# Ranks and counts of edges on TensorE with reads in runs, heads in two buffers, tiles evenly spaced, 858 gather columns

## The chip, the core and the metric

The kernel runs on one core of a Trainium2 chip. The metric is the device time of one execution in microseconds. TensorE multiplies, VectorE, ScalarE and GpSimd work on vectors, SyncE (SP) issues DMAs; each takes its instructions in order, and they wait for one another through semaphores. GpSimd issues the indirect DMAs (gathers and scatters of rows).

## The reference, cut to what matters

```
x: (6250, 256) f32; src, dst: (100000,) int32, sorted by dst; edge_weight: (100000,)
xn = layernorm(x)
agg = segment_sum(xn[dst] * edge_weight[:, None], src, 6250)
gnn = relu((xn + agg) @ W1 + b1) @ W2 + b2               # 256 -> 512 -> 256
k, v = per-head layernorms of xn (8 heads of 32, own weights and biases)
mix = per head q @ (k.T @ v / N), q = xn;  + xn
x = x + gnn + mix
z = layernorm(x)
top 2 of 16 experts of z @ gate_w + gate_b, softmax of the two values
moe = sum of weight * (relu(z @ w1[e] + b1[e]) @ w2[e] + b2[e])   # 256 -> 512 -> 256
out = x + layernorm(z + moe) * gamma + beta
```

## The kernel before, in words

Nodes are padded to 49 buckets of 128 rows (`NT`), a bucket being the high part of `src`. The kernel is a row of blocks; within a block each engine has its own program, and a barrier stands between blocks.

**First block.** The 100,000 edges lie in SBUF as 128 partitions by 28 groups of 28 (`EC` = 784 columns, written `(g j)`). `bkt_f` holds each edge's bucket. It is counted how many edges of each group fall in each bucket: VectorE makes for every bucket a 0/1 matrix of 784 columns (`matches`, L774), TensorE adds them up over partitions and positions with 28 matmuls of 196 columns for seven buckets (`count`, L628), VectorE copies the counts (L778). Each edge also needs its rank among the edges of the same partition, group and bucket: for every distance d from 1 to 27 GpSimd subtracts bucket numbers d positions apart (L591), ScalarE squares and applies relu(1 - x), so that equal buckets give 1 (L671, L675), GpSimd adds that to `rank` (L596). From the counts VectorE makes prefix sums, writes each edge's start by a predicated copy for every bucket (L859 mask, L862 copy of the starts, L867), adds `rank` (L874) and gets each edge's place. The edges are then sorted into records of eight (`QE`), group by group: VectorE builds matrices (`matrices`), ScalarE weights them and normalizes x, TensorE multiplies (L650), GpSimd scatters the records to DRAM (L606).

**Second block, the gather loop.** The records are `ET` = 864 columns of 128 edges, in 432 pairs. GpSimd gathers the 128 rows of xn of a column in one indirect DMA (L1278), twelve pairs of places in a ring; SP lets a pair go when its place is free (`release`, L1149). The other engines run in *units*: 480 of them (432 pairs, 48 of which are used twice where a pair crosses a bucket's end, rounded up to a multiple of 6). In a unit VectorE selects rows by edge (L1422, twice), TensorE multiplies (L1303, L1304), VectorE adds into the bucket's sums (L1439). TensorE may be four units ahead of VectorE (`SUMB`). Further work hangs on unit numbers, written into the program when it is generated:

- *heads*, seven groups of seven tiles at `heads_from[g]` = 9, 19, 29, 38, 48, 58, 68: xn is loaded into `xn_rows`, VectorE centres it into `nd` (`heads_centre`), ScalarE squares, VectorE sums, takes the root's inverse and scales (`heads_norm`, four units on), TensorE makes k.T v (`head_sums`, four units on, L1314), VectorE adds (`heads_add`, nine units on).
- *tiles* (slots), one for each of the 49 buckets, at `turn_unit[s]`, when the bucket's sums are done: transposes, MLP, attention, residual, norm, gate, choice of two experts over 13 units, then the ranks of the choices; ScalarE writes marks for the expert lists (`mark`, L1235 to L1238).

**Third block.** Lists of tokens by expert are made of the marks; SP loads weights of the first four experts (L1692, L1696). **Fourth block.** 114 tiles of 128 tokens go through their experts (gather L1842, TensorE L1863, L1884), SP loads the other twelve experts' weights. **Last block.** Mixing, norm, output.

Of the kernel before, what the change touches and what calls it, by code (L numbers as in the profile page):

```python
# [58 lines left out]
def gps_layer(nc, x, src, dst, edge_weight, gW1, gb1, gW2, gb2, klw, klb, vlw, vlb,  # L59
# [32 lines left out]
    ET = -(-(NGRP * ((GC * P + NT * (QE - 1)) // QE)) // (TQ * ROUND)) * ROUND  # L92
    EROUNDS = ET // ROUND

# [15 lines left out]
    assert EP % PB == 0 and RB <= BU  # L110
# [9 lines left out]
    rec_dram = nc.dram_tensor("edge_records_sorted", [ET * TQ + NGRP * NQ * P, QW], F32).ap()  # L120
# [10 lines left out]
    with ctx:  # L131
# [47 lines left out]
        apart = [early(EC) for _ in range(3)]  # L179
        early = carver(row_hot[1], GC * P)  # L180
        rank = early(EC)
        same = [early(EC) for _ in range(3)]
# [39 lines left out]
        starts = [carve(NGRP) for _ in range(4)]  # L222
# [3 lines left out]
        later = lambda a, d: bg2(a)[:, :, d:]  # L226
# [16 lines left out]
        edge_sel = edge_sel.rearrange("p (s n) -> p s n", n=P)  # L243
        tile_rows = nd[:, 0:BT * P * REC].rearrange("p (c s w) -> p c s w", c=BT, w=REC)
# [30 lines left out]
        zeros = carve(ET * REC)  # L275
# [194 lines left out]
        s_local = sem("local_ranks")  # L470
# [37 lines left out]
        with nc.Block() as block:  # L508
            @block.sync
            def _(sp):  # L510
# [11 lines left out]
                sp.dma_start(rec_dram[0:ET * TQ, :].rearrange("(p z) w -> p (z w)", p=P), zeros).then_inc(s_recz, 16)  # L522
# [35 lines left out]
            def _(pool):  # L558
# [13 lines left out]
                pool.iota(aside, pattern=[[NQ * P, NGRP]], base=ET * TQ, channel_multiplier=0,  # L572
# [12 lines left out]
                pool.memset(rank, 0.0).then_inc(s_local, 1)  # L585
                pool.wait_ge(s_bkt, 1)
                for d in range(1, GC + 2):
                    if d < GC:
                        if d > 3:
                            pool.wait_ge(s_same, d - 3)  # L590
                        pool.tensor_tensor(later(apart[d % 3], d), later(bkt_f, d), bg2(bkt_f)[:, :, 0:GC - d],  # L591
                                           ALU.subtract).then_inc(s_gap, 1)
                    if d >= 3:
                        pool.wait_ge(s_same, d - 2)
                        pool.wait_ge(s_local, d - 2)
                        pool.tensor_tensor(later(rank, d - 2), later(rank, d - 2), later(same[(d - 2) % 3], d - 2),  # L596
                                           ALU.add).then_inc(s_local, 1)

# [18 lines left out]
            def _(pe):  # L617

                pe.wait_ge(s_upto, 1)

                def count(j, k):
                    r, p, _ = tile_at(j, k)
                    pe.wait_ge(s_match, r * GT + GT)
                    if over(r - 1):
# [6 lines left out]
                run_steps(pe, count, 0, NR - 1, 1, (NR - 1) // 2)  # L631
# [35 lines left out]
            def _(act):  # L667

                for d in range(1, GC):
                    act.wait_ge(s_gap, d)  # L670
                    act.activation(later(apart[d % 3], d), later(apart[d % 3], d), ACT.Square).then_inc(s_gapsq, 1)  # L671
                    act.wait_ge(s_gapsq, d)
                    if d > 3:
                        act.wait_ge(s_local, d - 2)
                    act.activation(later(same[d % 3], d), later(apart[d % 3], d), ACT.Relu, bias=1.0, scale=-1.0).then_inc(s_same, 1)  # L675

# [62 lines left out]
            def _(dve):  # L739
# [17 lines left out]
                dve.wait_ge(s_dve, n.add(P // HD + 1))  # L757
                dve.tensor_copy(bkt_f, bkt_i).then_inc(s_bkt, 1)
                dve.wait_ge(s_bkt, 1)

                dve.tensor_scalar(src_i, src_i, P - 1, None, ALU.bitwise_and).then_inc(s_dve, 1)
                dve.wait_ge(s_dve, n.add())
                dve.scalar_tensor_tensor(code, dst_i, float(P), src_i, ALU.mult, ALU.add).then_inc(s_dve, 1)
                dve.wait_ge(s_dve, n.add())

                dve.wait_ge(s_consts, 8)
                dve.tensor_tensor(upto_b, before[:], ident[:], ALU.add).then_inc(s_upto, 1)

                def matches(j, k):
                    r, p, _ = tile_at(j, k)  # L770
                    if looped(r) or r < NR:

                        for i in range(GT):
                            dve.tensor_scalar(match[p][:, i * EC:(i + 1) * EC], bkt_f, iota_n[:, ds(r * GT + i, 1)], None,  # L774
                                              ALU.is_equal).then_inc(s_match, 1)
                    if over(r):
                        dve.wait_ge(s_counted, r)
                        dve.tensor_copy(cnt[:, ds((r - 1) * (GT * NGRP), GT * NGRP)],  # L778
                                        bank[1 - p][:, 0:GT * NGRP]).then_inc(s_cnt, 1)

                run_steps(dve, matches, 0, NR, 1, (NR - 1) // 2)


# [11 lines left out]
                dve.memset(restart, 1.0).then_inc(s_dve, 1)  # L795
                dve.wait_ge(s_dve, n.add())
# [1277 lines left out]
```

## Time and profile before

| | |
|---|---|
| three runs | 2380.33, 2381.49 (median), 2381.5 us |
| the profiled execution | 2381.34 us, span 2379.1 us |
| TensorE busy | 1638.3 us (69%), mean granted clock 0.849 |
| VectorE busy | 1453.1 us (61%) |
| GpSimd busy | 1391.3 us (58%) |
| ScalarE busy | 739.9 us (31%) |
| DMA | 233.44 MB, mean 98 GB/s |

The span is the time from the first to the last instruction of the profiled execution. Busy time is averaged over stages that have different limits, so the stretches are read one by one. A granted clock of 1.00 is TensorE at 2.4 GHz, 0.50 is 1.2 GHz.

### The profile page before, as it was taken

The page shows a single profiled execution, that of the slowest core. Times are in us where ns is not written, and L with a number is a line of the kernel's source. Part 1 is how long each engine was busy: PE and PEld are TensorE (multiplying, and loading weights), DVE is VectorE, ACT ScalarE, POOL GpSimd, SP SyncE. Part 2 cuts the span into 40 slices and gives each one's busy share as a digit, 9 for nine tenths or more (in the row PEclk, how much of TensorE's full clock was granted, in tenths as well). Part 3 has the DMA queues.
Part 4 walks back from the last instruction along what each step waited for, and adds up shares of the span by engine and source line. Part 5 has one row for each costly group of instructions (what it writes and reads, how often), then busy time and mean ns, then how long its engine had stood idle before and what let it go on. Part 6 is the DMA issues. An engine that isn't in the chain of part 4 may idle for free. (4 is left out here: it accounts for less than half of the span.)

```text
span 2379.1 us, 40341 instructions
## 1 busy us (share of the span) xinstructions
PE 1638.3 (69%) x9284; PEld 1371.2 (58%) x9285; DVE 1453.1 (61%) x4177; ACT 739.9 (31%) x2173; POOL 1391.3 (58%) x1512
## 2 busy tenths in 40 slices
PE   5602788624556887787878777776569999999900
PEld 2202777613555776676766656654468888888800
DVE  8499988637676666666665665654343443434379
ACT  4803789500000344322222222221213333333200
POOL 8001788748876776677777777776225554555400
PEclk9856899856778999898898889888679999999955
DMA  4000011254333444344444444447581111111184
GB/s 153 0 0 16 20 35 34 20 104 134 115 113 89 133 127 120 108 128 120 127 121 125 124 119 125 124 118 98 77 288 57 62 62 57 60 61 61 52 290 149
DMA packets 133498, 233.44 MB, mean 98 GB/s; under 512 B 28775, under 2 KB 85199, under 8 KB 133374
## 3 DMA queue, kind: packets, MB, share of 16 engines
q0 software_dynamic: 56384, 145.17, 22.8%
q1 hardware_dynamic: 49294, 61.00, 8.4%
q10 hardware_dynamic: 27696, 25.83, 3.4%
q8 instruction: 51, 0.84, 0.1%
q14 instruction: 73, 0.60, 0.1%
HBM read 189.48 MB, written 42.43 MB: 97 GB/s over the span
## 5 line engine op out<-in xcount | busy, mean ns | idle before, releaser
L1278 POOL DMA_INDIRECT lower<-xn_rows,lower x864 | 865.0, 1001 | 310.5 <-issue 239.3
L1303 PE MATMUL bank<-lower 128*128 x960 | 342.9, 443 | 145.4 <-SPq L1154 121.3
L1439 DVE TENSOR_TENSOR xh<-xh,bank 128x256 f32 x480 | 199.7, 416 | 285.9 <-PE bank L1304 285.1
L1422 DVE TENSOR_SCALAR lower<-iota_n,lower 128x128 f32<-128x128 f32 x960 | 294.4, 357 | 69.7 <-issue 56.2
L606 POOL DMA_INDIRECT edge_records_sorted<-lower x112 | 200.8, 1793 | 205.1 <-ACT lower L717 174.9
L1304 PE MATMUL bank<-lower 128*128 x960 | 320.5, 419 | 0.0
L1303 PEld LDWEIGHTS bank<-lower 128*128 128x128 f32 x960 | 177.7, 213 | 212.1 <-issue 200.0
L650 PE MATMUL bank<-lower 128*64 128x128 f32 x1568 | 189.8, 285 | 125.1 <-ACT lower L701 120.8
L650 PEld LDWEIGHTS bank<-lower 128*64 128x64 f32 x1568 | 183.6, 145 | 128.8 <-DVE lower L915 121.4
L1834 POOL DMA_INDIRECT expert_rows<-arena,dest_idx x114 | 114.6, 1005 | 213.7 <-DVE arena L1929 196.5
L1920 DVE TENSOR_SCALAR arena<-bank,b_tile 128x128 f32<-128x128 f32 x456 | 128.4, 344 | 178.4 <-PE bank L1863 178.4
L1863 PEld LDWEIGHTS bank<-arena 128*128 128x128 f32 x1824 | 225.9, 195 | 6.0
L1304 PEld LDWEIGHTS bank<-lower 128*128 128x128 f32 x960 | 206.1, 215 | 35.1
L1863 PE MATMUL bank<-arena 128*128 128x128 f32 x1824 | 226.3, 278 | 0.0
L1884 PE MATMUL bank<-upper,arena 128*128 x912 | 225.9, 391 | 0.0
L1884 PEld LDWEIGHTS bank<-upper,arena 128*128 128x128 f32 x912 | 165.3, 191 | 29.6 <-issue 3.6
L701 ACT ACTIVATE lower<-lower 128x32 f32<-128x32 f32 x784 | 169.3, 309 | 9.3 <-DVE lower L900 8.4
L1901 ACT ACTIVATE arena<-lower 128x1024 f32 x114 | 120.5, 1057 | 60.9 <-issue 60.9
L1929 DVE COPY arena<-bank 128x256 f32<-128x256 f32 x114 | 48.4, 424 | 144.0 <-PE bank L1884 144.0
L1907 ACT ACTIVATE arena<-bank 128x256 f32<-128x256 f32 x114 | 43.7, 383 | 289.4 <-PE bank L1873 289.4
L1842 POOL DMA_INDIRECT arena<-xn_rows,tok_idx x114 | 109.5, 960 | 38.7 <-issue 32.2
L1216 ACT ACTIVATE std<-mv,eps_col 128x1 f32<-128x1 f32 x49 | 14.4, 295 | 320.1 <-DVE mv L1589 319.0
(316 smaller groups left out, 2530.4 us busy)
## 6 DMA issues: line engine op xcount, KB each, us to landing
lower<-xn_rows,lower POOLq DMA_INDIRECT x864
lower<-in_L_ffn_w SPq DMA_DIRECT2D x16, 512.0 KB, 9.7
upper<-in_L_ffn_w SPq DMA_DIRECT2D x16, 512.0 KB, 10.5
xn_rows<-xh SPq DMA_DIRECT2D x7, 896.0 KB, 4.1
arena<-xn_rows ACTq DMA_DIRECT2D x7, 896.0 KB, 5.5
lower<-xn_rows ACTq DMA_DIRECT2D x49, 128.0 KB
xn_rows<-lower ACTq DMA_DIRECT2D x49, 128.0 KB
x_plus_beta<-lower ACTq DMA_DIRECT2D x49, 128.0 KB
```

Of the source, the lines that this page charges most:

```text
L606: pool.indirect_dma_start(rec_dram, bass.IndirectOffsetOnAxis(quad_idx[i][:, c:c + 1], 0), quads[i][:, c * QW:(c + 1) * QW], None).then_in ...
L650: mm = pe.matmul(bank[6 + p][0:NQ * QW, 0:P], moving[p][:, e].rearrange("p c w -> p (c w)"), row_hot[p][:, e, :], start=e == 0, stop=e == ...
L701: done = act.activation(moving[p][:, e, :, 1], col_hot[p][:, e, :], ACT.Copy, scale=group_wgt[p][:, e:e + 1])
L1278: pool.indirect_dma_start(edge_rows[:, t % ROUND, :], None, xn_dram, bass.IndirectOffsetOnAxis(source.bitcast(U32)[:, t:t + 1], 0)).then_i ...
L1303: pe.matmul(sums_at(u), edge_sel[:, 2 * u % ESEL, :], rows_flat[:, ds(at, D)], start=True, stop=False)
L1304: pe.matmul(sums_at(u), edge_sel[:, (2 * u + 1) % ESEL, :], rows_flat[:, ds(at + D, D)], start=False, stop=True).then_inc(s_sum, 1)
L1422: dve.tensor_scalar(edge_sel[:, (2 * u + h) % ESEL, :], iota_n[:], lane[:, at:at + 1], weight_s[:, at:at + 1], ALU.is_equal, ALU.mult).the ...
L1439: dve.tensor_tensor(xh[:, at], xh[:, at], sums_at(u), ALU.add).then_inc(s_acc, 1)
L1863: mm = pe.matmul(bank[2 + p][:, m * P:(m + 1) * P], w1_tile[p][:, c * F + m * P:c * F + (m + 1) * P], tokT[p][:, c * P:(c + 1) * P], start ...
L1884: mm = pe.matmul(bank[6 + p][:, 0:D], hidT[p][:, m * P:(m + 1) * P], upper[:, ds(e * (FC * D) + m * D, D)], start=False, stop=m == FC - 1)
L1901: act.activation(w1_tile[p], lower[:, ds(e * (DC * F), DC * F)], ACT.Copy).then_inc(s_w1t, 1)
L1920: dve.tensor_scalar(hidT[p][:, m * P:(m + 1) * P], bank[2 + p][:, m * P:(m + 1) * P], b1_tile[:, ds(t + m * XT, 1)], 0.0, ALU.add, ALU.max ...
```

## The change

**Counts.** A copy of the buckets in the order `(j g)`, `bkt_c`, is what the matches are made of. For one position c the count's matmul now reads 28 neighbouring elements for each of seven buckets; before it read elements 28 apart. The loops are written out.

```
-                    matched = match[p].rearrange("p (b g j) -> p b g j", g=NGRP, j=GC)
+                    matched = match[p].rearrange("p (b j g) -> p b j g", g=NGRP, j=GC)
                     for c in range(GC):
-                        mm = pe.matmul(bank[p][:, 0:GT * NGRP], upto_b, matched[:, :, :, c], start=c == 0, stop=c == GC - 1)
+                        mm = pe.matmul(bank[p][:, 0:GT * NGRP], upto_b, matched[:, :, c, :], start=c == 0, stop=c == GC - 1)
```

**Ranks.** GpSimd's subtractions and additions go. TensorE makes the difference of two positions as a sum of two matmuls, with the identity and with minus the identity, and adds the equal ones into banks 6 and 7; ScalarE reads the difference from PSUM.

```
+                def differences(d):
+                    if d > 2:
+                        pe.wait_ge(s_gapsq, d - 2)
+                    for h, lo, hi in halves_from(d):
+                        to = bank[2 + 2 * (d % 2) + h][:, 0:hi - lo]
+                        pe.matmul(to, ident_b, bkt_c[:, lo:hi], start=True, stop=False)
+                        mm = pe.matmul(to, minus_b, bkt_c[:, lo - d * NGRP:hi - d * NGRP], start=False, stop=True)
+                    mm.then_inc(s_gap, 1)
+                def add_same(d):
+                    pe.wait_ge(s_same, d)
+                    for h, lo, hi in halves_from(d):
+                        mm = pe.matmul(bank[6 + h][:, lo - h * EH:hi - h * EH], ident_b, same[d % 2][:, lo:hi],
+                                       start=False, stop=hi - lo == NGRP)
+                    mm.then_inc(s_local, 1)
...
+                differences(1)
+                differences(2)
+                for d in range(1, GC):
+                    add_same(d)
+                    if d + 2 < GC:
+                        differences(d + 2)
+                    if d % 4 == 3:
+                        count(d // 4)
```

```
-                    act.activation(later(apart[d % 3], d), later(apart[d % 3], d), ACT.Square).then_inc(s_gapsq, 1)
+                    if d > 2:
+                        act.wait_ge(s_same, d - 2)
+                    for h in range(2):
+                        lo, hi = max(d * NGRP, h * EH), (h + 1) * EH
+                        if lo < hi:
+                            sq_done = act.activation(apart[d % 2][:, lo:hi], bank[2 + 2 * (d % 2) + h][:, 0:hi - lo], ACT.Square)
+                    sq_done.then_inc(s_gapsq, 1)
```

On TensorE, at its program's start, `xh` holds the match matrices and `lower` the buckets and the rank matrices. Before:

```order
L628 MATMUL bank0<-xh,lower 128x196 [waits bucket_matches,prefix_matrix_made]
L628 MATMUL bank0<-xh,lower 128x196 x27
L628 MATMUL bank1<-xh,lower 128x196 [waits bucket_matches]
L628 MATMUL bank1<-xh,lower 128x196 x27
L435 UNCONDITIONAL_BRANCH
```

and now, from the differences of distance 4 over the addition of distance 3 and the differences of distance 5 to the first count (the numbers of lines are those of the changed kernel):

```order
L627 MATMUL bank2<-lower 128x280 [waits bucket_gaps_squared]
L628 MATMUL bank2<-lower 128x280
L627 MATMUL bank3<-lower 128x392
L628 MATMUL bank3<-lower 128x392
L634 MATMUL bank6<-lower 128x308 [waits same_buckets]
L634 MATMUL bank7<-lower 128x392
L627 MATMUL bank4<-lower 128x252 [waits bucket_gaps_squared]
L628 MATMUL bank4<-lower 128x252
L627 MATMUL bank5<-lower 128x392
L628 MATMUL bank5<-lower 128x392
L645 MATMUL bank0<-xh,lower 128x196 [waits bucket_matches]
L645 MATMUL bank0<-xh,lower 128x196 x27
```

A count of 28 matmuls stands behind every fourth distance, and each distance waits for ScalarE (`same_buckets`, `bucket_gaps_squared`).

**VectorE of the first block.** The scans' restart columns are written by GpSimd at the start, not by VectorE between its steps. The loop over buckets is written out and reads the starts in place (no L862). The ranks are added from the two banks in two instructions.

```
-                            dve.tensor_copy(starts[k % 4], start[:, ds((r * GT + k) * NGRP, NGRP)]).then_inc(s_dve, 1)
...
+                        dve.copy_predicated(bg2(pos), bg2(masks[(b - 1) % 4]), start[:, (b - 1) * NGRP:b * NGRP].unsqueeze(2)
+                                            .to_broadcast([P, NGRP, GC])).then_inc(s_dve, 1)
```

**Columns.** `ET` is 858, not 864; the zeroed part of the records stays 864 columns (`ZT`). There are 429 pairs and still 480 units.

```
-    ET = -(-(NGRP * ((GC * P + NT * (QE - 1)) // QE)) // (TQ * ROUND)) * ROUND
-    EROUNDS = ET // ROUND
+    ET = -(-(NGRP * ((GC * P + NT * (QE - 1)) // QE)) // (2 * TQ)) * 2
+    ZT = -(-ET // 8) * 8
```

**Heads.** Groups use `nd` and `xn_rows` in turn, and are centred in place; a group is loaded when the sums of the group two before are done. TensorE's sums come eight units on, VectorE's addition thirteen.

```
+        head_rows = lambda g: nd if g % 2 else xn_rows
-                            if u == heads_from[g] + 4 + k // 2:
+                            if u == heads_from[g] + 8 + k // 2:
                                 head_sums(g, k)
-                        if u == heads_from[g] + 9:
+                        if u == heads_from[g] + 13:
                             heads_add(g)
```

**Tiles.** They begin at units 88, 96, 103, 111, 118, ..., 7.5 apart until tile 34, where before they began at 88, 93, 98, 102, 107, ..., 4.67 apart until tile 15; from 34 on the numbers are the same (343, 352, ...), the last 482. `stage_h` comes one unit earlier, `mark` two units later and behind the unit's other work; the last `mark` goes to the third block, beside VectorE's work there.

```
-        turn_unit = [max(slots_from + 1 + -(-14 * s // 3), done_by[s + 1] + 2) for s in range(NT)]
+        turn_unit = [max(slots_from + 1 + -(-15 * s // 2), done_by[s + 1] + 2) for s in range(NT)]
```

**Weights.** In the third block SP loads one expert's weights, and the next four in the fourth, when the second token tile has landed.

```
-                for e in range(WAHEAD):
-                    sp.dma_start(w1_sb[:, e], w1[e].rearrange("(c p) f -> p c f", p=P)).then_inc(s_we[e], 16)
...
+                sp.dma_start(w1_sb[:, 0], w1[0].rearrange("(c p) f -> p c f", p=P)).then_inc(s_we[0], 16)
...
+                    if e == 0:
+                        sp.wait_ge(s_tok[1], 16)
+                        for later in range(1, WAHEAD):
+                            load_weights(sp, later)
```

On SP, before, around the barrier into the fourth block (`lower` holds w1, `upper` w2):

```order
L1692 DMA lower<-in_L_ffn_w 128x2x512 x4
L1696 DMA upper<-in_L_ffn_w 128x4x256 [waits tiles_listed] x4
L1807 UNCONDITIONAL_BRANCH [waits barrier_Pool_Activation_PE_DVE_SP_release]
L1685 DMA lower<-in_L_ffn_w 128x2x512 [waits weights_of_expert0]
L1686 DMA upper<-in_L_ffn_w 128x4x256
```

and now:

```order
L1720 DMA lower<-in_L_ffn_w 128x2x512
L1722 DMA upper<-in_L_ffn_w 128x4x256 [waits tiles_listed]
L1839 UNCONDITIONAL_BRANCH [waits barrier_Pool_Activation_PE_DVE_SP_release]
L1714 DMA lower<-in_L_ffn_w 128x2x512 [waits weights_of_expert0,rows_landed1]
L1715 DMA upper<-in_L_ffn_w 128x4x256
L1714 DMA lower<-in_L_ffn_w 128x2x512
```

Six of the eight transfers stand behind the barrier and behind the landing of the second token tile (`rows_landed1`).

## Rows read from the trace of the kernel before

**Rows 1.** The page's first line.
```profile
span 2379.1 us, 40341 instructions
```
**Rows 2.** Time line of TensorE to 250 us: start us, us, engine, line.
```profile
35.46 56.70 PE L628 MATMUL bank<-xh,lower 128*128 128x196 bf16 x168 [0.49 <-DVE xh L774]
92.71 1.92 PE L638 MATMUL bank<-xh,lower 128*128 128x476 f32 x2 [0.55 <-DVE xh L778]
```
**Rows 3.** Busy us (instructions) of PE, PEld, DVE, ACT, POOL; clock; DMA.
```profile
540.00:760.00 220.00, 124.83 (x579) 107.30 (x579) 149.35 (x295) 13.62 (x14) 167.22 (x139) 0.75 0.37 113
860.00:1000.00 140.00, 110.85 (x609) 93.95 (x606) 92.01 (x379) 56.32 (x154) 87.33 (x93) 0.91 0.40 117
1000.00:1630.00 630.00, 490.29 (x2304) 395.98 (x2305) 385.82 (x1484) 159.52 (x443) 478.36 (x498) 0.88 0.42 123
```
**Rows 4.** Waits (us in total, times, longest): 1000:1630, then 540:760 twice, 860:1000.
```profile
POOL lower L1278 <- SPq L1149: 11.0, 36, 0.3
...
POOL lower L1278 <- SPq L1149: 13.6, 12, 4.1
...
PE bank L1314 <- DVE lower L1470: 92.2, 7, 16.5
...
POOL lower L1278 <- SPq L1149: 29.5, 18, 5.4
```
**Rows 5.** Time line of TensorE near the gather loop's end.
```profile
1684.07 1.22 PE L1303 MATMUL bank<-lower 128*128 x2 [2.11 <-SPq L1154]
...
1687.40 1.22 PE L1303 MATMUL bank<-lower 128*128 x2 [1.26 <-SPq L1154]
```
**Rows 6.** Time line of TensorE in the third block.
```profile
1732.05 0.21 PE L1712 MATMUL bank<-lower,upper 128*128 128x114 bf16 x1
1732.10 0.21 PE L1711 MATMUL bank<-lower,upper 128*128 128x114 bf16 x1
```
**Rows 7.** Time line of ScalarE: ranks, and a copy from PSUM later.
```profile
12.09 0.83 ACT L671 ACTIVATE lower<-lower 128x756 f32<-128x756 f32 x1 [10.01 <-POOL lower L591]
...
64.03 0.26 ACT L671 ACTIVATE lower<-lower 128x28 f32<-128x28 f32 x1
...
1664.80 0.38 ACT L1222 ACTIVATE lower<-bank 128x256 f32<-128x256 f32 x1 [1.19 <-PE bank L1364]
```
**Rows 8.** Time line of VectorE in the first block.
```profile
104.83 1.20 DVE L795 MEMSET xh<- 128x1372 f32 x1 [0.35 <-DVE xh L792]
...
137.57 0.42 DVE L859 TENSOR_SCALAR xh<-lower,iota_n 128x784 uint16<-128x784 bf16 x1 [0.25 <-DVE upper L848]
...
139.33 0.41 DVE L859 TENSOR_SCALAR xh<-lower,iota_n 128x784 uint16<-128x784 bf16 x1
139.66 0.17 DVE L862 COPY xh<-xh 128x28 f32 x1
139.74 1.02 DVE L867 COPY_PREDICATED xh<-xh 128x784 f32<-128x784 uint16 x1
140.66 0.41 DVE L859 TENSOR_SCALAR xh<-lower,iota_n 128x784 uint16<-128x784 bf16 x1
...
147.70 0.42 DVE L859 TENSOR_SCALAR xh<-lower,iota_n 128x784 uint16<-128x784 bf16 x1 [0.46 <-DVE xh L867]
```
**Rows 9.** Time line of VectorE: additions of two units without waits.
```profile
527.43 0.41 DVE L1439 TENSOR_TENSOR xh<-xh,bank 128x256 f32 x1
...
528.27 0.41 DVE L1439 TENSOR_TENSOR xh<-xh,bank 128x256 f32 x1
```
**Rows 10.** Time line of ScalarE at the second block's end.
```profile
1716.58 0.40 ACT L1235 ACTIVATE upper<-iota_n,upper 128x128 f32<-128x128 f32 x1 [4.69 <-DVE upper L1639]
...
1718.80 0.48 ACT L1238 ACTIVATE upper<-upper 128x128 f32 x1
```
**Rows 11.** Time lines of GpSimd and TensorE at the fourth block's start.
```profile
1742.89 0.97 POOL L1842 DMA_INDIRECT arena<-xn_rows,tok_idx  x1 [0.82 <-POOL tok_idx L1828]
...
1750.21 0.66 PE L1873 MATMUL bank<-ident,arena 128*128 128x128 f32 x2 [11.05 <-DMA arena<-xn_rows,tok_idx]
```

More of the change, by code:

```diff
@@ L109, in gps_layer @@
     BT = -(-ET // P)
[L110 removed]
+    assert RB <= BU and ZT * TQ % P == 0
     WAHEAD = 4
@@ L581, in _ @@
                                    pattern=[[0, P]], channel_multiplier=1).then_inc(s_consts, 1)
[L585 to L597, printed above, removed]
+                for a, first in ((restart_g, bg(restart_g)[:, :, 0:1]), (restart_b, gb(restart_b)[:, :, 0:1])):
+                    pool.memset(a, 1.0).then_inc(s_poolc, 1)
+                pool.wait_ge(s_poolc, 6)
+                for a, first in ((restart_g, bg(restart_g)[:, :, 0:1]), (restart_b, gb(restart_b)[:, :, 0:1])):
+                    pool.memset(first, 0.0).then_inc(s_restart, 1)
                 def scatter(r, i):
@@ L617, in _, with halves_from @@
             def _(pe):
-                pe.wait_ge(s_upto, 1)
-                def count(j, k):
-                    r, p, _ = tile_at(j, k)
+                pe.wait_ge(s_bkt, 2)
+                pe.wait_ge(s_upto, 3)
+                def halves_from(d):
+                    return [(h, max(d * NGRP, h * EH), (h + 1) * EH) for h in range(2) if d * NGRP < (h + 1) * EH]
+                def differences(d):
[6 more added lines that the diff above has]
+                    mm.then_inc(s_gap, 1)
@@ L629, in count @@
                     mm.then_inc(s_counted, 1)
-                run_steps(pe, count, 0, NR - 1, 1, (NR - 1) // 2)
+                for h in range(2):
+                    cols = slice(h * EH, (h + 1) * EH)
+                    pe.matmul(bank[6 + h][:, 0:EH], ident_b, bkt_c[:, cols], start=True, stop=False)
+                    pe.matmul(bank[6 + h][:, 0:EH], minus_b, bkt_c[:, cols], start=False, stop=False)
+                differences(1)
[6 more added lines that the diff above has]
+                        count(d // 4)
@@ L876, in _ @@
+                dve.wait_ge(s_dve, n.back(0))
+                dve.wait_ge(s_local, GC - 1)
+                for h in range(2):
+                    cols = slice(h * GC // 2, (h + 1) * GC // 2)
+                    dve.tensor_tensor(by_column(pos_i)[:, cols, :], by_column(pos)[:, cols, :],
+                                      bank[6 + h][:, 0:EH].rearrange("p (j g) -> p j g", g=NGRP), ALU.add).then_inc(s_dve, 1)
+                dve.wait_ge(s_dve, n.add(2))
                 dve.tensor_scalar(part_i, pos_i, QSHIFT, P - 1, ALU.arith_shift_right, ALU.bitwise_and).then_inc(s_dve, 1)
@@ L1245, in _ @@
                 load(0)
-                with act.Fori(0, NG - 1) as g:
+                for g in range(NG):
                     heads(g)
-                heads(NG - 1)
                 act.wait_ge(s_kv, DC)
```

187 lines of the change are left out of this document (96 added, 91 removed).

## The prediction

> **What bounds the kernel now.** I read the page first, then the time lines of each engine in the first stage, the busy time by stretch, and the waits in the gather loop. The profiled execution has a span of 2379.1 us [rows 1] and took 2381.34 us, 2.2 us more than its span; the median of the three runs shown is 2381.49 us, so the sum below, made against 2381.3, stands for the median too. No engine bounds the whole; the stages follow each other and each has its own limit.
>
> In the first stage TensorE counts: 168 matmuls of 196 columns run without a break from 35.46 to 92.16 us, 0.337 us each, and the prefix matmuls start at 92.71 us [rows 2]. VectorE only builds what they read; GpSimd and ScalarE make the ranks meanwhile and are done near 64 us, off the path. From 92.7 us to the sort at 220 us VectorE alone sets the pace.
>
> In the gather loop (512 to 1698 us) GpSimd sets the pace. From 1000 to 1630 us it issues 498 gathers, one per 1.265 us [rows 3], and its 36 waits for a free place come to 11.0 us, 0.30 us each, which is what issue costs anyway [rows 4]. In three places it waits longer. From 540 to 760 us (the heads) 12 such waits hold 13.6 us, 10.0 above issue, and TensorE stands 92.2 us in seven waits for the normed heads [rows 4]. From 860 to 1000 us (tiles at every 4.67 units) 18 waits hold 29.5 us, 24.1 above issue [rows 4]. At the end a pair of gathers is used every 3.33 us instead of 2.53 [rows 5].
>
> **First stage.** The new count reads 7 runs of 28 neighbouring elements where the old one took single elements 28 apart. The trace has no such read. Bounds: a bf16 matmul on 114 neighbouring columns starts every 0.05 us [rows 6], 0.44 ns a column, twice that at the half clock, so 196 columns cost 0.086 or 0.17 us; at the other end stands the old read, 0.337 us [rows 2]. I take the run price, since 27 of 28 steps go to the next element: 196 matmuls in 17 us.
>
> The Trainium skill, page "SBUF — State Buffer", section "Door 1: The DMA port swizzle", says that reads which hit one 16-byte line at least twice run at full bandwidth and that each step to a new line pays. The old read's 0.337 us [rows 2] agrees with it; by that rule the new read is cheap and the time is the forecast's, and if each of its columns paid as before it would be about 2342 us.
>
> New on TensorE are the ranks: for each of 27 distances the difference of bucket numbers (two matmuls, in two halves) and the addition (one). The widths 784-28d add up to 10,584; three times that and 4 x 392 is 33,320 columns, with the counts 71,736: 31.5 us at the full clock, 60 at the half. ScalarE squares from two banks and applies Relu. From 0.83 us for 756 columns and 0.26 for 28 an instruction is 0.24 us and 0.78 ns a column, and reading a bank is no dearer (0.38 us for 256) [rows 7]: 67 instructions, 32.7 us. The engines hand over at every distance. Distances 1 to 13 are ScalarE's: 39 x 0.24 us + 15,288 x 0.78 ns = 21.3 us. From 14 on ScalarE has 11.3 us and TensorE, with four of the seven counts, 13.5; a narrow distance is shorter than a count, so little overlaps: 14 to 25 us. TensorE can start at about 12.2 us. At the full clock the stage ends between 48 and 58 us; I take 58, with the handovers. At the half clock TensorE alone needs 60, and the stage ends at 72 to 83, say 80. TensorE is busy two thirds of it; a stretch with 57% busy shows clock 0.75 and one with 79% shows 0.91 [rows 3], so I take 0.82 and an end at 62. Against 92.7 that is **-30.7** (-12 to -35). VectorE's 49 matches, 0.41 us each like the bucket loop's comparisons [rows 8], are hidden behind the counts; without that cover a round of seven would cost 2.9 us.
>
> Behind it VectorE loses two memsets of 1.20 us and two small ones [rows 8]: **-2.6**, with nothing beside them. The loop over the buckets starts a round of seven every 10.13 us (137.57 to 147.70), with 1.33 us from bucket to bucket and a stall at each round's end [rows 8]. Without the copy of the start (0.08 us from its start to the next) a bucket is 1.25 us, and no round ends: 49 x 1.25 + 0.5 instead of 7 x 10.13, less 0.3 for the addition that is now two: **-8.8**. The sort and all up to the gathers move forward unchanged.
>
> **Gather loop.** Heads: TensorE comes to the head sums at unit 8 behind the centring, not 4, and leads VectorE by four units at most, so the norm (unit 4) is done when it comes. The 92.2 us of waits go, and **-10** of GpSimd's with them. VectorE's long instructions stay, and so, I think, does the dearer gather there (167.22/139 = 1.20 us against 478.36/498 = 0.96 [rows 3]). The earlier group's products are added at unit 13, which is the next group's third or fourth, before its sums; the load waits for the buffer two groups back, long summed. If a buffer came late, the 10 us would return.
>
> Tiles: at 4.67 units GpSimd runs out of places; at 9.75 (1000 to 1630) never. The new 7.5 lies between. From 860 to 1000 us 93 gathers are 51.7 units [rows 3], 2.71 us a unit, 12.7 us a tile. A unit alone costs VectorE 0.84 us [rows 9], so a tile 8.8 us. At 7.5 units that is 15.1 of the 17.1 us that GpSimd needs for its 13.5 gathers: it fits with 12% to spare, for 34 tiles instead of 16. I leave 2 us of waits: **-22** (0 to -24). Tiles from 34 on stand where they stood, so the last ends no later.
>
> Columns: 858 instead of 864 are three pairs fewer, at the end, where a pair costs 3.33 us [rows 5]: **-10** (not below 3 x 2.53 = 7.6). There are still 480 units; the last three repeat a pair.
>
> **End of the loop and experts.** The last marks on ScalarE run from 1716.58, where VectorE's last instruction lets them go, to 1719.28 us, the end of the block [rows 10]. Moved past the barrier they lie beside VectorE's making of the high places: **-2.7**, and if that cover failed nothing is lost, for they would stand where they do now. One expert's weights are loaded there instead of four. The first token gather is issued by 1743.86 us and used at 1750.21 [rows 11], with the weights of twelve experts under way. Without them at most some 4 of these 6.35 us go; the three experts' weights that come later lie beside the first tiles and take some of it back. Net **-2** (-6 to +5).
>
> Sum: 30.7 + 2.6 + 8.8 + 10 + 22 + 10 + 2.7 + 2 = 88.8, and 2381.3 - 88.8 = 2292.5, said as **2293 us**.
>
> **Rivals.**
> 1. The clock stays at half in the first stage. For it: TensorE and ScalarE take turns, and a stretch with breaks shows 0.75 [rows 3]; against it: the breaks are under 2 us each, and the loop's stretches with such breaks show 0.9. The stage ends at 80, not 62: 2311 us. The Trainium skill ("TensorE: Matmul & The Clock Gate", "What's actually happening") has the array held at half by default and released by activity; it allows either here, and no row decides.
> 2. Runs cost as much as single elements: 196 x (0.337 - 0.086) = 49 us more, 2342 us. For it: no row has a broken run. Against it: the 0.05 us of [rows 6].
> 3. At 7.5 units the loop is still full. If a unit cost 2 us instead of 0.84, a tile would cost 3.3, and 7.5 units 18.3 us against 17.1: 1.2 us lost on each of 33 tiles, 40 us of waits in place of 2. Half of that is likelier: the 22 us are given back, 2315 us.
> 4. The late weights hold the experts up. Expert 1 is wanted some seven tiles on; if its weights or the tokens beside them delay the tiles by 10 us net: 2305 us.
> 5. Slower than before: broken runs cost more than single elements, because each of the seven runs restarts the read. It decides from 0.086 + 88/196 = 0.54 us a matmul; at 0.60 the time is 2394 us. No matmul of 196 columns in the trace costs more than the old one's 0.337 us.
>
> **How the numbers follow.** The forecast with its own spread (2280 to 2304) gets 0.63, rival 1 0.10, rival 2 0.06, rival 3 0.09, rival 4 0.07, rival 5 0.02, and 0.03 is left for what I have not seen. The range 2278 to 2325 holds the forecast, rivals 1 and 4 and most of rival 3, and leaves out 2, 5 and the rest. A difference of 0.2% (4.8 us) is about what can be told from none. Faster by more: 0.97; within it: 0.01; slower: 0.02.
>
> **What would show it.** Count matmuls near 0.09 us and the prefix matmuls at about 62 us; the bucket loop in 62 us; no wait for normed heads on TensorE; a gather every 1.27 us from the end of the heads to the last columns, without waits for places; 858 gathers; no ScalarE instruction behind VectorE's last at the barrier; the first token used in about 3 us. I am wrong if the counts cost 0.3 us, if the granted clock of the first stage is near 0.5, or if waits for places come back between tiles.

## The result, and the profile after

The changed kernel takes 2280.89 us (median of four runs, 2278.57 to 2282.12) where the old one takes 2380.91 in the same job: a ratio of 0.9584, with a 95% interval of 0.9567 to 0.9602. That is 100 us less; 88.8 were forecast. The profiled execution took 2280.35 us with this span:

```profile
span 2278.6 us, 40242 instructions
```

Of TensorE in the first stage, the time line (start us, us, engine, line) answers to [rows 2]:

```profile
43.24 2.52 PE L645 MATMUL bank<-xh,lower 128*128 128x196 bf16 x28
...
46.78 0.25 PE L634 MATMUL bank<-lower 128*128 128x168 bf16 x1 [0.57 <-ACT lower L710]
...
51.10 2.52 PE L645 MATMUL bank<-xh,lower 128*128 128x196 bf16 x28
54.24 1.04 PE L667 MATMUL bank<-xh,lower 128*128 128x476 f32 x2 [0.62 <-DVE xh L814]
```

28 counts in 2.52 us are 0.090 us each, against 0.337 before. The prefix matmuls start at 54.24 instead of 92.71. The same stretch in the view of windows (busy us and instructions of PE, PEld, DVE, ACT, POOL; granted clock; DMA share; GB/s) and in the groups by line (count, busy us, mean ns, idle ahead):

```profile
12.00:54.00 42.00, 34.65 (x318) 26.05 (x316) 19.15 (x55) 29.22 (x81) 0.00 (x0) 1.00 0.50 148
```
```profile
L805 DVE TENSOR_SCALAR xh<-lower,iota_n 128x784 bf16<-128x784 bf16 x49 | 16.8, 417 | 0.0
L710 ACT ACTIVATE lower<-lower 128x756 bf16<-128x756 bf16 (+26 forms) x27 | 14.3, 530 | 0.9
...
L634 PE MATMUL bank<-lower 128*128 128x392 bf16 (+13 forms) x40 | 9.1, 284 | 7.0 <-ACT lower L710 6.8
```

The clock is 1.00, TensorE is busy 34.65 of 42 us, and its waits for ScalarE are 6.8 us in all. (The trace's first record of the clock begins at 15.95 us; ahead of it the view reads 1.00 for want of a record, and matmuls of 392 columns start 0.33 us apart there, 0.17 later: the half clock.) VectorE behind it, to be read beside [rows 8]:

```profile
93.61 0.76 DVE L883 TENSOR_SCALAR xh<-lower,iota_n 128x784 uint16<-128x784 bf16 x2
...
95.21 0.41 DVE L883 TENSOR_SCALAR xh<-lower,iota_n 128x784 uint16<-128x784 bf16 x1
...
154.90 1.64 DVE L896 TENSOR_TENSOR xh<-xh,bank 128x392 int32<-128x392 f32 x2
```

With the copies between them that is a bucket every 1.25 us and no break: the loop takes 61.3 us. In the gather loop, first the waits of GpSimd from 540 to 760 us, then from 860 to 1000, beside [rows 4]:

```profile
POOL lower L1305 <- SPq L1174: 2.7, 9, 0.3
...
POOL lower L1305 <- SPq L1174: 4.3, 14, 0.3
```

Both are 0.3 us a wait, what issue costs. The windows answer to [rows 3]:

```profile
1000.00:1500.00 500.00, 387.92 (x1959) 311.20 (x1957) 315.51 (x1233) 142.03 (x402) 378.90 (x398) 0.94 0.43 127
...
1540.00:1580.00 40.00, 23.51 (x88) 16.91 (x89) 14.86 (x55) 6.22 (x18) 22.04 (x24) 0.78 0.93 88
```

In the last 40 us of gathers DMA is busy 0.93 of the time and moves less (88 GB/s) than at 0.43 before: something else is slow there. GpSimd's and ScalarE's time lines from there to the third block, which is GpSimd's iota:

```profile
457.32 0.95 POOL L1305 DMA_INDIRECT lower<-xn_rows,lower  x1 [0.30 <-issue]
...
1576.95 0.94 POOL L1305 DMA_INDIRECT lower<-xn_rows,lower  x1 [0.30 <-issue]
1616.45 0.24 POOL L1726 IOTA lower<- 128x114 f32 x1 [38.57 <-POOLq L1149]
1639.21 0.18 POOL L1864 CAST tok_idx<-rows_all 128x1 uint32<-128x1 f32 x1 [22.51 <-POOLq L1717]
1640.21 0.97 POOL L1878 DMA_INDIRECT arena<-xn_rows,tok_idx  x1 [0.82 <-POOL tok_idx L1864]
```
```profile
1594.13 0.40 ACT L1265 ACTIVATE upper<-iota_n,upper 128x128 f32<-128x128 f32 x1 [0.31 <-issue]
...
1596.35 0.48 ACT L1268 ACTIVATE upper<-upper 128x128 f32 x1
1596.73 0.40 ACT L1228 ACTIVATE lower<-xh 128x256 f32 x1
...
1610.42 0.48 ACT L1268 ACTIVATE upper<-upper 128x128 f32 x1
1610.81 0.36 ACT L1252 ACTIVATE lower<-bank 128x256 f32<-128x256 f32 x1
...
1651.07 1.06 ACT L1937 ACTIVATE arena<-lower 128x1024 f32 x1 [4.38 <-SPq L1843]
```

Two things show that I had not foreseen. Marks (L1265 to L1268) run right ahead of the last tile's staging of h (L1228) and of its last norm's copy (L1252), which start the moment they end. And ScalarE waits 4.38 us at 1651.07 for SP's word that an expert's weights are there.

Read at the same places of both traces, the difference adds up like this (negative is saved):

| stretch | before | after | difference |
|---|---|---|---|
| start to the prefix matmuls | 92.71 | 54.24 | -38.5 |
| from there to the first sort matrix | 120.3 | 106.3 | -14.0 |
| from there to the first gather (512.03, 457.32) | 299.1 | 296.8 | -2.2 |
| gathers 0 to 166 | 255.9 | 241.4 | -14.5 |
| gathers 166 to 250, 350 to 830 | 715.4 | 709.4 | -6.0 |
| gathers 250 to 350 | 149.2 | 126.0 | -23.2 |
| gather 830 to the last's end | 54.5 | 43.7 | -10.8 |
| last gather's end to the third block | 32.4 | 38.6 | +6.2 |
| third block | 22.3 | 22.8 | +0.5 |
| fourth block's start to the end of the span | 637.2 | 639.4 | +2.2 |

The sum is -100.3; the spans differ by 100.5.

### The profile page after: what moved, and what is told of

Its sections match the earlier page's. It is cut to its first block and busy times, and to the rows that moved or that the text cites. A ratio compares the mean times of both kernels' runs of the same rounds, so it can differ in the third digit from the quotient of the medians.

```text
span 2278.6 us, 40242 instructions
## 1 busy us (share of the span) xinstructions
PE 1603.1 (70%) x9408; PEld 1348.5 (59%) x9409; DVE 1416.2 (62%) x4128; ACT 731.0 (32%) x2186; POOL 1326.7 (58%) x1455
## 5 line engine op out<-in xcount | busy, mean ns | idle before, releaser
L1305 POOL DMA_INDIRECT lower<-xn_rows,lower x858 | 850.6, 991 | 270.2 <-issue 238.5
L1330 PEld LDWEIGHTS bank<-lower 128*128 128x128 f32 x960 | 169.2, 209 | 318.3 <-issue 307.9
L1331 PEld LDWEIGHTS bank<-lower 128*128 128x128 f32 x960 | 204.3, 213 | 35.3
L1943 ACT ACTIVATE arena<-bank 128x256 f32<-128x256 f32 x114 | 43.8, 384 | 285.1 <-PE bank L1909 285.1
## 6 DMA issues: line engine op xcount, KB each, us to landing
upper<-in_L_ffn_w SPq DMA_DIRECT2D x16, 512.0 KB, 10.5
```

Source lines behind the costliest of these rows:

```text
L1305: pool.indirect_dma_start(edge_rows[:, t % ROUND, :], None, xn_dram, bass.IndirectOffsetOnAxis(source.bitcast(U32)[:, t:t + 1], 0)).then_i ...
L1330: pe.matmul(sums_at(u), edge_sel[:, 2 * u % ESEL, :], rows_flat[:, ds(at, D)], start=True, stop=False)
L1331: pe.matmul(sums_at(u), edge_sel[:, (2 * u + 1) % ESEL, :], rows_flat[:, ds(at + D, D)], start=False, stop=True).then_inc(s_sum, 1)
```

## The experiments

Ratios are against the kernel before in the same job. Where I give a difference from the changed kernel I also compare profiled spans, since two jobs' medians differ by a few us.

**The count's read.** The change with matches laid out as before:

```
-  match[..] = (bkt_c == b)          matched = match "p (b j g) -> p b j g";  moving = matched[:, :, c, :]
+  match[..] = (bkt_f == b)          matched = match "p (b g j) -> p b g j";  moving = matched[:, :, :, c]
```

> The changed kernel, with its counts read as before: the matches are laid out group by group, so each count matmul takes 196 single elements 28 apart instead of seven runs of 28. All else stays. My theory, that the read sets the price of a count: 196 matmuls cost 0.337 instead of about 0.087 us, 49 us more on a TensorE that is busy 40 of the stage's 43 us, so the prefix matmuls start near 103 us and the time is about 2330 us (2322 to 2335). Rival: the old stage was long because GpSimd's ranks slowed VectorE's matches and kept TensorE waiting, and the read was not the limit; then the stage ends before 75 us and the time is below 2301 us.

2341.22 us, ratio 0.9819 (0.9793 to 0.9844); the span is 59 us above that of the changed kernel. TensorE's time line, and the window of its end:

```profile
86.60 9.62 PE L645 MATMUL bank<-xh,lower 128*128 128x196 bf16 x28
...
107.63 1.93 PE L667 MATMUL bank<-xh,lower 128*128 128x476 f32 x2 [0.62 <-DVE xh L814]
```
```profile
92.00:106.00 14.00, 13.42 (x47) 5.29 (x46) 1.81 (x3) 8.83 (x40) 0.00 (x0) 0.50 0.00 0
```

The stage ends at 107.6, 53.4 us later, of which the read is 49; the rest is the ranks' matmuls at a lower clock. Up to the first gather another 5.3 us come in: 2.5 behind the prefix matmuls, which still run at the half clock, and 2.8 in the sort, for which I have no cause. The rival is out: the read alone decides whether this stage lasts 54 or 108 us.

**Runs of four.** The groups are split into seven times four, so that a matmul reads 49 runs of 4 neighbours:

```
+  bkt_q = copy of bkt_i, "p (h g j) -> p h j g", g=4;  match[..] = (bkt_q == b)
+  matched = match "p (h j g) -> p h j g", g=4;         moving = matched[:, :, c, :]
```

> The changed kernel, with matches laid out so that a count matmul reads 49 runs of 4 neighbours; one more copy of the bucket numbers (about 1 us) on VectorE. Theory A: each step to an element that is no neighbour costs the 0.337/196 = 1.7 ns of the old read, each step to a neighbour 0.44 ns; then a matmul costs 0.044 * 147/100 + 49 * 1.7 / 1000 = about 0.15 us, and the time is 2281 + 196 * 0.063 + 1 = about 2294 us. Theory B: whatever is read in runs of at least 8 bytes goes at full rate: 0.087 us and 2282 us. Theory C: the read is slow as soon as runs are short: 0.3 us and 2323 us.

2290.87 us, ratio 0.9601 (0.9575 to 0.9627). The count in TensorE's time line:

```profile
28.94 2.70 PE L646 MATMUL bank<-xh,lower 128*128 128x196 bf16 x28
```

28 in 2.70 us are 0.096 us a matmul, against 0.090 in runs of 28 and 0.344 without runs: for the read theory B holds but for 0.006 us, and A and C fall. The Trainium skill, page "SBUF — State Buffer", table row "Cachelines", asks for at least two hits in a 16-byte line; four neighbours of two bytes meet it, and 0.096 us agrees. The total is some 9 us above theory B's: the stage ends at 57.72, 3.5 us later (TensorE starts 2.1 us later behind the added copy, and 196 x 0.006 is 1.2), and the rest, in the sort and the gathers, has no cause that I can name. Over all my runs, but for those of the slow chip below (up to 294), the sort alone took 278 to 283 us from the first scatter to the first gather.

**Counts without the ranks.** The kernel before, only its count changed:

```
+  bkt_c = copy of bkt_i, "p (g j) -> p j g"
-  matches from bkt_f, matched[:, :, :, c]
+  matches from bkt_c, matched[:, :, c, :]      (ranks stay on GpSimd and ScalarE)
```

> The kernel before, with the counts alone changed: bucket numbers are copied into the order column by column, matches follow it, and a count matmul reads seven runs of 28. The ranks stay on GpSimd and ScalarE. My theory now: VectorE's matches cost 1.1 to 1.5 us each while GpSimd makes the ranks and 0.35 us after, so they become the limit and the prefix matmuls start near 72 us instead of 92.7; the time is about 2360 us, and the other 18 us of the changed stage belong to the ranks' move. Rival A, the counts alone explain the stage: it ends near 56 us and the time is 2344 us. Rival B, the read was no limit: 2376 us or more.

2363.35 us, ratio 0.9911 (0.9885 to 0.9937). VectorE's time line, TensorE's wait from 12 to 72 us, TensorE's time line at the end:

```profile
15.78 20.88 DVE L776 TENSOR_SCALAR xh<-lower,iota_n 128x784 bf16<-128x784 bf16 x14
...
63.75 3.18 DVE L776 TENSOR_SCALAR xh<-lower,iota_n 128x784 bf16<-128x784 bf16 x7
```
```profile
PE bank L629 <- DVE xh L776: 43.8, 6, 27.2
```
```profile
70.06 1.04 PE L639 MATMUL bank<-xh,lower 128*128 128x476 f32 x2 [0.54 <-DVE xh L780]
```

A match costs VectorE 1.49 us beside GpSimd's rank operations and 0.45 when they thin out. TensorE now waits 43.8 us for matches, 27.2 of them ahead of its first count, and the stage ends at 70.06: 22.7 us come from the counts alone, the other 15.8 of the 38.5 from moving the ranks, which frees VectorE.

**Tiles.** `turn_unit` with 14/3 in place of 15/2:

> The changed kernel with the tiles again at every 14/3 units behind the first, all else kept. My theory: GpSimd runs out of places in the first 16 tiles as before, 23 us come back in waits: about 2303 us (2300 to 2306), with gathers 250 to 350 taking 149 us instead of 126. Rival: the gain of the even spacing was in part the other edits' (fewer columns, VectorE's shorter operations), and less than 12 us come back: 2293 us or less.

2305.63 us, ratio 0.9671 (0.9645 to 0.9696); the span is 20.1 us longer. Gathers 250 to 350 take 141.3 us instead of 126.0, and GpSimd's waits for places from 800 to 950 us are back:

```profile
POOL lower L1305 <- SPq L1174: 21.0, 19, 5.1
```

The term stands at 15 us, between theory (23) and rival (under 12). The rest of the 20 lies mostly where the tiles' spacing does not reach: 1.6 us ahead of the first gather, 1.6 in the gathers behind 830 and 2.3 among the experts. Before the change the gathers 250 to 350 took 149.2, so that some 8 of their 23 us belong to other edits; which, no run shows.

**The unused records.** The list's end is filled ahead of the sort with zero records, which all name source row 0. Here they name rows 0, 1, 2, ... with weight zero:

```
   pool.wait_ge(s_zero, 1)
+  pool.iota(zeros "p (r w) -> p r w"[:, :, 0], pattern=[[P, ZT]])      # code = 128 * row
```

> The changed kernel, with the unused records at the end of the sorted list naming the source rows 0, 1, 2, ... (weight still zero) where they all named row 0; one more iota on GpSimd in the first stage. The last 28 gathers of the changed kernel take 43.7 us where 28 of the steady ones take 35, DMA is busy 0.97 of that time and moves only 79 GB/s. My theory: that is the price of 128 reads of one row, and with spread rows the last gathers go at GpSimd's pace and their rows land sooner: 2281 - 8.5 - 3 = about 2269 us (2265 to 2273). Rival: it is the number of descriptors or other traffic, and nothing changes: 2281 us.

2264.55 us, ratio 0.9513 (0.9497 to 0.9529), 16.3 us less than the changed kernel. The window of the last gathers of this kernel, then of the changed one:

```profile
1534.00:1569.00 35.00, 27.18 (x129) 21.54 (x129) 17.27 (x68) 6.61 (x19) 26.51 (x28) 0.91 0.40 118
```
```profile
1534.00:1578.00 44.00, 26.18 (x112) 19.25 (x110) 17.42 (x67) 6.62 (x19) 26.63 (x28) 0.81 0.91 94
```

The same 28 gathers take 34.8 us and not 43.7, with no wait, at a DMA share of 0.40 and not 0.91; and from the last gather's start to the third block it is 30.5 us instead of 39.5. The slow end of both kernels was 128 reads of one row in each gather, and its landing. It gave more than I expected.

**The marks.** On ScalarE:

```
   f(s)
+  if s == NT - 1 and f in (copy_turned, relu):
+      mark(NT - 3 if f is copy_turned else NT - 2)
...
-  if u - 4 in rank_unit[:-1]:
+  if u - 4 in rank_unit[:-3]:
```

> The changed kernel, with the marks of the third and second tile from the end placed on ScalarE behind the copy and the relu of the last tile, where it waits for TensorE anyway, and not ahead of the last tile's staging of h. My theory: in the changed kernel the staging stands 2.2 to 5 us behind those marks, and the copy of the last norm another 1.3 us: about 2277 us (2274 to 2279), with 35 to 37 us from the last gather to the third block in place of 39.5. Rival: the last tile waits for the rows of the last gathers, not for ScalarE, and the time stays at 2281 us.

2278.04 us (2274.34 to 2282.69), ratio 0.9574 (0.9558 to 0.9590): against the changed kernel's interval not to be told from no change. The trace is clearer. ScalarE's time line:

```profile
1593.26 0.42 ACT L1228 ACTIVATE lower<-xh 128x256 f32 x1 [1.12 <-DVE xh L1470]
...
1604.36 0.38 ACT L1252 ACTIVATE lower<-bank 128x256 f32<-128x256 f32 x1 [1.49 <-PE bank L1395]
```

Both wait for their real inputs now, 3.5 and 6.5 us earlier than in the changed kernel, and from last gather to third block it is 33.5 us instead of 39.5. The kernel before took 33.3 there, so the 2.7 us that the last mark should have saved do not show even now.

**The weights.** Four experts loaded in the third block, as before the change:

```
+  for e in range(WAHEAD): load w1[e];  for e in range(WAHEAD): wait for the lists, load w2[e]
-  if e == 0: wait_ge(s_tok[1], 16); load_weights(1..3)          (fourth block)
```

> The changed kernel, with the weights of four experts loaded in the third block as before, all else kept. The two traces say that from the fourth block's start to the end the changed kernel takes 639.4 us where the old one took 637.2. Theory A: the late weights (ScalarE waits 4.4 and 1.9 us for them in the first tiles) cost more than the free queues give to the first tokens, and the old way is better: about 2278.5 us. Theory B, the step of my prediction: the late weights save 2 us net: about 2283 us. Neither is far above what a run tells apart; the first tokens' times will say which.

2275.17 us, ratio 0.9554 (0.9538 to 0.9569); the medians differ by 5.7 us (the intervals of the two ratios just touch), the spans by 3.8, and the fourth block to the end takes 635.1 us. TensorE's time line, first for this kernel, then for the changed one:

```profile
1647.23 0.66 PE L1908 MATMUL bank<-ident,arena 128*128 128x128 f32 x2 [11.35 <-DMA arena<-xn_rows,tok_idx]
```
```profile
1643.21 0.66 PE L1909 MATMUL bank<-ident,arena 128*128 128x128 f32 x2 [7.78 <-DMA arena<-xn_rows,tok_idx]
...
1652.27 3.75 PE L1899 MATMUL bank<-arena 128*128 128x128 f32 x16 [2.16 <-ACT arena L1937]
```

The first token is 3.6 us later behind its block's start, as my prediction had it, but at the thirteenth tile's weight copy the kernel with early weights is 4.5 us ahead (65.7 against 70.2 us from the block's start, by the time lines of ScalarE). Theory A holds.

**The heads.** One buffer for loaded rows and one for centred, sums four units behind, additions nine:

```
-  head_rows = lambda g: nd if g % 2 else xn_rows
-  u == heads_from[g] + 8 + k // 2        ->  + 4
-  u == heads_from[g] + 13                ->  + 9
```

> The changed kernel, with the heads as before: one buffer for loaded rows and one for centred, sums four units behind, additions at unit 9. My theory: TensorE waits for the normed heads again and GpSimd 10 us for places; with the dearer gathers that went in the same stretch 12 to 15 us come back: 2294 us (2291 to 2297). Rival: with the earlier start of the loop and other edits, the waits no longer reach GpSimd: 2281 to 2284 us.

2300.33 us (2293.73 to 2303.30), ratio 0.9652 (0.9632 to 0.9672). The waits from 500 to 720 us:

```profile
PE bank L1338 <- DVE lower L1494: 96.0, 7, 20.7
...
POOL lower L1302 <- SPq L1173: 20.3, 15, 4.2
```

TensorE's waits for the normed heads are back (92.2 in [rows 4]). Gathers 100 to 166 take 109.5 us, 18.3 more than in the changed kernel: 13.1 of wait and 5.2 of dearer gathers. The medians differ by 19 us, more than the 12 to 15 expected.

**Three edits together**, the rows spread, the marks moved, four experts' weights early; a form of it with two experts' weights; and the change with 864 columns, in one job:

> The changed kernel with three edits of the earlier runs together: source rows spread over the unused records, the marks of the third and second last tile behind the last tile's copy and relu, and four experts' weights loaded in the third block. Alone they gave 16, 3 to 6 and 4 to 6 us. If they add up, about 2256 us (2252 to 2260). Rival: with spread rows the last tile is late for another reason (the places of the last gathers are no limit and ScalarE is free earlier), the marks' gain is gone, and the time is 2260 us or more.

> As the run with three edits, but only the first two experts' weights are loaded in the third block, the next two behind the second tokens. Theory: ScalarE's two waits in the changed kernel are for experts 1 and 2, so the first of them goes, and the first tokens come 2 us sooner than with four: within 2 us of the run with four. Rival: any weight that is loaded beside the first token gathers delays some tile, and it is 3 us slower than with four.

> The changed kernel with 864 columns again, the six more read row 0 only. By the end of the changed kernel's loop (a pair every 3.3 to 3.5 us) three pairs more cost about 10 us: 2291 us. Rival: the last pairs' rows land in a queue that is full already and the six cost only GpSimd's 1.25 us each, 7.5 us: 2288 us; or they are hidden behind the last tiles: below 2285 us.

2501.16 us, 2505.50 us and 2518.85 us, against 2605.04 for the kernel before: ratios 0.9614 (0.9581 to 0.9647), 0.9622 (0.9583 to 0.9662) and 0.9690 (0.9645 to 0.9735). The chip of this job was 9% slower with every kernel. The window of the steady loop, which in the changed kernel elsewhere issues 81 gathers in 100 us, and GpSimd's time line, for the kernel with three edits:

```profile
1100.00:1200.00 100.00, 72.85 (x344) 61.46 (x343) 54.02 (x215) 25.82 (x74) 61.59 (x66) 0.84 0.35 104
```
```profile
807.93 0.94 POOL L1310 DMA_INDIRECT lower<-xn_rows,lower  x1 [2.21 <-SPq L1177]
```

66 gathers, with waits for places, at a DMA share of 0.35: what makes the places late I have not found. It is not the gathers' own packets: worked out as in the last section they take 0.15 us each (29.8% of 16 engines for 3120 packets in these 100 us), as in the changed kernel (35.9% for 3808). So the job says nothing certain of differences of 10 us. In its traces ScalarE waits 2.29 us once with two experts' weights and never with four, but at the thirteenth tile's weight copy both stand 67.1 us from the block's start, as theory has it; their medians differ by 4.3 us, which their intervals do not tell apart. The columns stay open as an experiment. The first kernel once more:

> The same kernel as the run with three edits. In that job every kernel, the one before too, ran about 9% longer: the gather loop, whose gathers follow each other every 1.26 us elsewhere, took 1.55 us a gather and waited for places all along. Once more, beside the kernel before: where that takes about 2381 us, this should take about 2256 us (2252 to 2260) if the three gains add up, and 2260 or more if the marks' gain is gone once the rows are spread.

2255.31 us (2254.90 to 2258.33), ratio 0.9479 (0.9461 to 0.9497): 25.6 us below the changed kernel, where the three alone gave 16.3, 2.9 and 5.7, together 24.9. They add up. GpSimd's time line:

```profile
1567.66 0.95 POOL L1310 DMA_INDIRECT lower<-xn_rows,lower  x1 [0.30 <-issue]
1593.30 0.23 POOL L1734 IOTA lower<- 128x114 f32 x1 [24.70 <-POOLq L1152]
```

25.6 us from the last gather to the third block, 39.5 in the changed kernel, 33.3 before.

## Why the prediction was right, and where it was not

The direction and the mechanism of nearly every step held, and 2280.9 lies in the range, near its lower end. That the sum is only 11.5 us off is in part luck, since misses cancel: five terms were too small, by 16.9 us together, two too large, by 13.1, and 7.7 us net came where nothing was forecast, 6.0 of them in the rest of the gather loop and 2.2 in the sort, without a cause that a run shows. Step by step:

- **First stage, -30.7 forecast, -38.5 measured, below the bound of -35.** The run price was right (0.087 forecast, 0.090 measured; the run with the old layout shows what the other price would do). Two sizes were off. I took the clock as 0.82 from stretches of the gather loop with a similar busy share; it was 1.00 from 15.95 us on. No row of the kernel before could tell: its first stage ended at the half clock (last section), and my 0.82 stood between two levels that no row decided. And for distances 14 to 27 I took the upper end of my 14 to 25 us, handovers included; they took about 18. The bound of -35 was too tight by my own working, which had the stage end between 48 and 58 us at the full clock; it ended at 54. I also left out that VectorE's matches cost 1.49 us while GpSimd works and 0.35 us when it doesn't. The third experiment shows it as the hidden limit: without the ranks' move the stage ends at 70. So GpSimd's ranks, which I had called off the path, would have set its length through VectorE's matches as soon as the counts were fast.
- **VectorE behind it, -11.4 forecast, -14.0 measured.** The bucket loop gave 9.2 (8.8). The memsets' 2.6 came with 2.0 us of prefix matmuls, which I had not counted: the first of them ran at the half clock before and at the full one now. No experiment undoes this step; it rests on the two time lines.
- **Heads, -10 forecast, -14.5 measured.** The waits went (10.5 us in gathers 100 to 166). I kept the dearer gathers there at their old price; they cost 5.7 us less, and gathers 0 to 100 took 1.7 us more. The undoing brought 19 back.
- **Tiles, -22 forecast, -23.2 measured** in their gathers. The waits went as worked out, but that the size fits is in part luck: undoing the spacing alone brings 15 us back in these gathers, and 8 came from other edits.
- **Columns, -10 forecast, -10.8 measured**, by the traces alone: the experiment ran on the slow chip. The price of 3.33 us a pair was read right from [rows 5] but its reason was not asked for: reading one row 128 times. With spread rows three pairs would save 3 x 2.49 us.
- **Marks past the barrier, -2.7 forecast, +6.2 measured from the last gather to the third block.** The step failed. The last mark did leave the block, but the same edit put the two marks ahead of it in front of the last tile's work on ScalarE, and I costed the last mark alone. Moving them gives 6.0 us of the trace back, which leaves the stretch where it was before the change, and not 2.7 us shorter.
- **Experts' start, -2 forecast, +2.2 measured.** The sign of this step was wrong, inside its -6 to +5. The first token came 4 us sooner (3.0 us from gather to use instead of 7.3), and the weights of the next experts, each used for few tiles, came too late. I had put expert 1 some seven tiles on without a row for it; the waits stand at the second and third tile.
- **Rivals.** The clock did not stay at half; runs did not cost as much as single elements; the loop was not full at 7.5 units; rival 4 was true in kind, at 4 us instead of 12.

## What to carry to other kernels

Ask of every read on a hot path how many neighbours it takes at a time, and of every padding which address it names: the first cost 49 us here beside the other edits and 23 alone, the second 16, and neither shows in an instruction's shape. When work is moved off the end of a queue, cost everything that moved with it at its new place: the last tile's chain is where a few us on an idle engine become a few us of the time. And when one engine's stage is made faster, look for the engine that was hidden under it.

## What the runs showed of the hardware

- A bf16 matmul that moves 196 single elements 56 bytes apart takes 0.34 us at a granted clock of 1.00 and of 0.50 alike: the read sets its pace, not the array. In the first experiment the clock fell in the middle of 28 of them. The time line, and the windows of these matmuls ahead of the fall and behind it (PE, PEld, clock, DMA share, GB/s):

```profile
35.28 9.59 PE L645 MATMUL bank<-xh,lower 128*128 128x196 bf16 x28
...
35.30:41.00 5.70, 5.70 (x18) 1.95 (x18) 1.00 0.01 3
41.10:44.60 3.50, 3.50 (x12) 1.13 (x10) 0.50 0.00 0
```

Over that run's seven counts the matmuls start 0.335 us apart at 1.00 and 0.336 at 0.50, and the 28 from 86.60 us, all of them at 0.50, take 9.62 us. In runs of 28 the pace goes with the clock: 0.084 us from start to start at 1.00 and 0.162 at 0.50 in the third experiment. (The 0.090 and 0.096 us above, for runs of 28 and of 4, are at 1.00 and hold the last one's end as well.)

- In the old stage no clock is recorded: its trace's first record begins at 96.74 us, and windows ahead of it read 1.00 for want of one. What the array had there is seen from the prefix matmuls:

```profile
94.42 1.79 PE L639 MATMUL bank<-xh,lower 128*128 128x476 f32 x2
96.01 1.33 PE L638 MATMUL bank<-xh,lower 128*128 128x476 f32 x2
97.18 0.96 PE L639 MATMUL bank<-xh,lower 128*128 128x476 f32 x2
```

Two take 1.79 us and, behind 96.74, 0.96; in the first experiment two take 1.93 at 107.63 us, where 0.50 is recorded. So the old stage ended at the half clock, after nothing but strided counts. In the first experiment the clock rose four times while TensorE made ranks (17.18, 34.25, 47.91, 61.56 us) and fell each time in the middle of the strided counts behind them (24.01, 41.08, 54.73, 64.97), though TensorE was busy all around the falls (5.70 of 5.70 us and 3.50 of 3.50 in the windows above); with the counts in runs it stayed at 1.00 from 15.95 to 63.73 us, past the stage's end.

- A gather of 128 rows that are all the same row: DMA is busy 0.91 of the time at 94 GB/s, against 0.40 at 118 for distinct rows. From the views of the DMA queues, GpSimd's queue takes 16 x 0.893 x 36 / 1016 = 0.51 us a packet with one row and 16 x 0.358 x 26 / 985 = 0.15 us with distinct ones.

Their rows, queue by queue (packets, MB, share of 16 engines), changed kernel from 1540 to 1576 us:

```profile
q0 software_dynamic: 1016, 2.79, 89.3%
```

and with spread rows from 1540 to 1566 us:

```profile
q0 software_dynamic: 985, 2.71, 35.8%
```

- VectorE's compare of 784 bf16 elements took 0.35 us alone and 1.49 us beside GpSimd's two-input operations. In the third experiment, GpSimd's time line and VectorE's:

```profile
15.67 1.84 POOL L597 TENSOR_TENSOR lower<-lower 128x756 f32<-128x756 f32 x1
...
15.78 1.96 DVE L776 TENSOR_SCALAR xh<-lower,iota_n 128x784 bf16<-128x784 bf16 x1
```

GpSimd's ends at 17.51 us, the compare at 17.74; the first 14 compares end each 0.22 us behind one of 14 GpSimd additions and subtractions in a row, and in the kernel before the first 35 end 0.22 or 0.23 us behind one too. The Trainium skill, page "SBUF — State Buffer", section "A bandwidth-pool intuition that's wrong (but worth ruling out)", calls this a lock on a shared port and not a sharing of bandwidth; compares that end just behind GpSimd's instructions agree with a lock.
